# Five products of the self-attention and feed-forward parts in three rounded rounds, and w_down loaded later

## The reference

```python
x = x + xattn(layernorm(x), ctx_1024)      # q, k each layernormed by head, softmax, projection
x = x + attn(layernorm(x))                 # causal; scores plus 0.35 * tanh(Q) J tanh(K)
x = x + ffn(layernorm(x))

# attn: the three projections
Q = heads(Wq, bq); K = heads(Wk, bk); V = heads(Wv, bv)
# ffn: shared part and router
shared_out = silu(x @ shared_gate_w) * (x @ shared_up_w) @ shared_down_w
router_probs = softmax(x_flat @ router_w)
topk_probs, topk_idx = top_k(router_probs, 2)
# routed part: 16 experts, each silu(x @ g) * (x @ u) @ d, weighted by its probability
```

## Time and profile before

| | |
|---|---|
| timed executions | 1392.45, 1395.54, 1396.56 us; median 1395.54 us |
| the profiled execution's own time | 1382.54 us |
| its span (first to last instruction of the engines) | 1380.7 us |
| granted TensorE clock, mean over the span | 0.955 |
| PE busy | 1240.6 us (90%) |
| DVE busy | 984.4 us (71%) |
| ACT busy | 698.1 us (51%) |
| POOL busy | 450.4 us (33%) |

### The profile page before, as it was taken

The page is one execution under the profiler, slowest core; times in us unless marked ns, Lnnn a source line. Parts: engine busy times, 40 slices in busy tenths (PEclk is TensorE's granted clock), DMA queues, the critical chain, the costliest instruction groups (busy, mean ns, idle before and its releaser), DMA issues.

```text
span 1380.7 us, 54869 instructions
## 1 busy us (share of the span) xinstructions
PE 1240.6 (90%) x22808; PEld 1024.0 (74%) x22808; DVE 984.4 (71%) x2498; ACT 698.1 (51%) x1377; POOL 450.4 (33%) x436
## 2 busy tenths in 40 slices
PE   3789999999999999999999999999999986699950
PEld 3677878888888878788878787888888864488840
DVE  7458777777777777777777777777777763365547
ACT  1345555555555555555555555555555542255520
POOL 1322333333333333333333333333333222155530
PEclk7789999999999999999999999999999998699985
DMA  4100111111111111103111100111111002586558
GB/s 155 39 21 4 48 49 49 49 49 49 49 49 51 56 44 51 34 30 100 33 34 33 36 29 28 34 33 34 34 38 33 15 14 63 157 245 188 163 188 262
DMA packets 82579, 92.12 MB, mean 67 GB/s; under 512 B 17248, under 2 KB 72544, under 8 KB 82016
## 3 DMA queue, kind: packets, MB, share of 16 engines
q1 hardware_dynamic: 70816, 65.41, 16.4%
q0 software_dynamic: 6912, 19.01, 3.8%
q10 hardware_dynamic: 4608, 4.20, 0.9%
HBM read 61.19 MB, written 33.78 MB: 69 GB/s over the span
## 4 chain that ended last, share of the span: by engine, by line
PE 82%; DVE 9%; issue 4%; DMA 2%; ACT 1%; POOL 1%; SPq 0%; DVEq 0%; POOLq 0%; ACTq 0%
PE ringB L489 16%; PE ringC L500 14%; PE oA L582 10%; PE banksS L565 9%; DVE mx L1220 6%; PE banksS L783 5%; PE banksS L529 4%; PE ringB L663 3%; PE ringB L617 2%; PE ringB L649 2%; PE banksS L634 2%; PE ringB L484 2%; DMA out<-ksq 2%; PE oA L489 2%; PE banksS L544 2%
## 5 line engine op out<-in xcount | busy, mean ns | idle before, releaser
L863 ACT ACTIVATE pt<-banksS 128x1024 f32<-128x1024 f32 x128 | 127.7, 1023 | 129.6 <-PE banksS L565 118.0
L1039 POOL TENSOR_TENSOR kn<-kc,rr 128x512 f32<-128x512 f32 x64 | 66.6, 1062 | 336.0 <-DVE rr L1208 336.0
L500 PE MATMUL ringC<-wx_kv,ct 128*128 128x256 f32 x512 | 159.9, 312 | 13.6 <-DVE ws_down L1362 6.2
L1220 DVE TENSOR_REDUCE mx<-banksS 128x8 f32<-128x2048 f32 x64 | 146.3, 2287 | 0.9 <-PE banksS L544 0.9
L500 PE MATMUL ringC<-wx_kv_rest,ct 128*128 128x256 f32 x512 | 146.8, 287 | 0.0
L500 PE MATMUL ringC<-wx_kv,ct_rest 128*128 128x256 f32 x512 | 146.0, 285 | 0.0
L1033 POOL TENSOR_TENSOR sc<-sc,rz 128x1024 f32<-128x1024 f32 x32 | 62.3, 1948 | 223.5 <-DVE rz L1281 223.5
L565 PE MATMUL banksS<-qT,kT 17*128 17x64 f32 x4096 | 132.4, 278 | 0.9 <-DVE qT L1225 0.9
L565 PEld LDWEIGHTS banksS<-qT,kT 17*128 17x128 f32 x4096 | 123.5, 191 | 7.9 <-issue 1.4
L500 PEld LDWEIGHTS ringC<-wx_kv,ct 128*128 128x128 f32 x512 | 99.3, 194 | 27.6 <-DVE pos_u L1338 7.8
L1234 DVE RECIPROCAL rz<-oA 128x128 f32<-128x128 f32 x64 | 61.3, 957 | 55.5 <-PE oA L582 55.5
(11 more groups left out here) (219 smaller groups left out, 2957.0 us busy)
## 6 DMA issues: line engine op xcount, KB each, us to landing
ct_in<-in_ctxT SPq DMA_DIRECT2D x64, 256.0 KB, 3.1
pt<-rows_by_expert SPq DMA_DIRECT2D x80, 130.0 KB, 2.4
rows_by_expert<-in_pad_rows SPq DMA_DIRECT2D x16, 260.0 KB
xt<-in_x SPq DMA_DIRECT2D x32, 128.0 KB, 3.5
rows_without_experts<-base SPq DMA_DIRECT2D x32, 128.0 KB
pt<-expert_rows SPq DMA_DIRECT2D x16, 256.0 KB, 4.1
kn<-expert_rows SPq DMA_DIRECT2D x16, 256.0 KB, 4.2
out<-ksq ACTq DMA_DIRECT2D x32, 128.0 KB, 3.8
```

The lines of the kernel that those rows point to most:

```text
L500: mm = pe.matmul(ringC[:, half * DIM:(half + 1) * DIM], left[:, p, k, j // 2, (j % 2) * P:(j % 2 + 1) * P], right[:, k, part * DIM:(part + ...
L863: act.activation(pt[:, g, :, :, :, :].rearrange("p i q c n -> p i (q c n)"), banksS[:, :, g * 256:(g + 1) * 256], ACT.Exp)\
L1039: pool.tensor_tensor(kn[:, 2 * jj:2 * jj + 2, :, 0:HD].rearrange("p j h d -> p (j h) d"), kc[:, 2 * jj:2 * jj + 2, :].rearrange("p j (h d) ...
L1220: dve.tensor_reduce(mx[:, 2 * r:2 * r + 2, :, HD].rearrange("p q i -> p i q"), banksS[:, :, :].rearrange("p i (q m) -> p i q m", q=2), AX. ...
```

## The change

`x1T`, `hT`, `wa_qk`, `wa_v`, `w_route` and `ws_gu` become pairs of a rounded part (type fp32r) and a rest. The four products that read them (five weight matrices: q and k, v, the router, shared gate and up) go through `split_product`: six matmuls of fp32r instead of two of float32. DVE gets two new instructions in each step, `self_rows_rest` after `maxima` 0 and `ffn_rows_rest` after `key_sums` 1, which subtract the rounded rows from the PSUM bank. `free["NT"]` and `free["HT"]` are now raised by these; ACT's copy raises the new signals `rounded["NT"]` and `rounded["HT"]` on the same semaphore. The weights come into buffers used later (`sc`, `qkn`, `qk4`) and DVE splits them at the start of step 3. For the room, `w_down` now lies over `kn` and `kT`: SP loads it after the last use of these, in step 34, and DVE halves it in step 36. Rows that the last stage kept in `kn` and `kT` go elsewhere.

```diff
-        wa_qk = sb("wa_qk", [P, KD, 2 * DIM])
-        wa_v = sb("wa_v", [P, KD, DIM])
+        wa_qk, wa_qk_rest = (sb(n, [P, KD, 2 * DIM], F32R) for n in ("wa_qk", "wa_qk_rest"))
+        wa_v, wa_v_rest = (sb(n, [P, KD, DIM], F32R) for n in ("wa_v", "wa_v_rest"))
...
+        kn_kT = sb("kn_kT", [P, 2, 2048])
+        w_down = kn_kT[:, :, :].rearrange("p a (e d) -> p (a e) d", d=DIM)
...
+        rounded = {}
+        for u in ("NT", "HT"):
+            rounded[u], free[u] = Event(free[u].sem, 1, 2), Event(free[u].sem, 2, 2)
...
-                if 6 <= s < 18:
-                    load_expert_weights(s - 6)
+                if 6 <= s < 14:
+                    load_expert_weights(s - 2)
...
+                if s == TILES + 2:
+                    sp.wait_ge(full["C1"].sem, full["C1"].of(TILES - 1))
+                    for piece in range(4):
+                        load_expert_weights(piece)
...
+            def split_product(bank_, u, t, left, left_rest, source, right, right_rest, n):
+                pe.wait_ge(rounded[source].sem, rounded[source].of(t))
+                for r in (right, right_rest):
+                    for k in range(KD):
+                        pe.matmul(bank_[:, 0:n], left[:, k, :], r[:, k, 0:n], start=(r is right and k == 0), stop=False)
+                pe.wait_ge(free[source].sem, free[source].of(t))
+                for k in range(KD):
+                    mm = pe.matmul(bank_[:, 0:n], left_rest[:, k, :], right[:, k, 0:n], start=False, stop=(k == 1))
+                mm.then_inc(full[u].sem, 1)
...
-                product(bankB("QK"), "QK", lambda k: x1T[:, k, :], wa_qk, 2 * DIM)
+                split_product(bankB("QK"), "QK", b, x1T, x1T_rest, "NT", wa_qk, wa_qk_rest, 2 * DIM)
...
+            def self_rows_rest(b, p):
+                dve.wait_ge(rounded["NT"].sem, rounded["NT"].of(b))
+                freed(dve, full["QK"], b)
+                freed(dve, full["VP"], b)
+                dve.tensor_tensor(x1T_rest[:, :, :].rearrange("p k n -> p (k n)"), bankB("NT")[:, 0:DIM],
+                                  x1T[:, :, :].rearrange("p k n -> p (k n)").bitcast(F32), ALU.subtract).then_inc(free["NT"].sem, 1)
...
-                if s == TILES + 2:
+                if s == TILES + 4:
                     dve.wait_ge(expert_weights_in, 16 * 12)
                     dve.tensor_scalar(w_down[:, :, :], w_down[:, :, :], 0.5, None, ALU.mult).then_inc(weights_set, 1)
-                if s == 2:
+                if s == 3:
                     dve.wait_ge(self_weights_in, 16 * 7)
+                    split = ((wa_qk, wa_qk_rest, wa_qk_in), (wa_v, wa_v_rest, wa_v_in), (ws_gu, ws_gu_rest, ws_gu_in), (w_route, w_route_rest, w_route_in))
+                    for whole, _, source in split:
+                        ins = dve.tensor_copy(whole[:, :, :], source)
+                    ins.then_inc(setup_dve, 1)
+                    dve.wait_ge(setup_dve, 9)
+                    for whole, rest, source in split:
+                        dve.tensor_tensor(rest[:, :, :], source, whole[:, :, :].bitcast(F32), ALU.subtract)
                     dve.tensor_scalar(jmix[:, :, :], jmix[:, :, :], cols[:, 4:5], None, ALU.mult)
...
                 on(s, odd, 2, keys, 0)
                 on(s, odd, 3, maxima, 0)
+                on(s, odd, 4, self_rows_rest)
                 on(s, odd, 2, cross_normalised)
...
+                on(s, odd, 5, ffn_rows_rest)
                 on(s, odd, 2, queries)
```

More of the change, by code:

```diff
@@ L125, in perceiver_block @@
         w_gu = sb("w_gu", [P, KD, E, 2 * F])
-        w_down = sb("w_down", [P, E, DIM])
         wmean = sb("wmean", [P, KD, 3 * H])
@@ L163, in perceiver_block @@
         x1b = sb("x1b", [P, DIM])
-        x1T = sb("x1T", [P, KD, P])
+        x1T, x1T_rest = (sb(n, [P, KD, P], F32R) for n in ("x1T", "x1T_rest"))
         qkn = sb("qkn", [P, 2, H, PAD])
@@ L180, in perceiver_block @@
         h = sb("h", [P, 2, 2, ROW])
-        hT = sb("hT", [P, KD, P])
+        hT, hT_rest = (sb(n, [P, KD, P], F32R) for n in ("hT", "hT_rest"))
         th = sb("th", [P, DIM])
@@ L372, in load_self_weights @@
             def load_self_weights():
-                for dst, name in ((wa_qk, "wa_qk"), (wa_v, "wa_v"), (w_route, "w_route"), (ws_down, "ws_down")):
-                    load(dst[:, :, :], halves(name), self_weights_in)
-                load(ws_gu[:, :, 0:DIM], halves("ws_gate"), self_weights_in)
-                load(ws_gu[:, :, DIM:2 * DIM], halves("ws_up"), self_weights_in)
+                for dst, name in ((wa_qk_in, "wa_qk"), (wa_v_in, "wa_v"), (w_route_in, "w_route"), (ws_down[:, :, :], "ws_down")):
+                    load(dst, halves(name), self_weights_in)
+                load(ws_gu_in[:, :, 0:DIM], halves("ws_gate"), self_weights_in)
+                load(ws_gu_in[:, :, DIM:2 * DIM], halves("ws_up"), self_weights_in)
                 load(jmix[:, :, :], w["jmix"], self_weights_in)
@@ L640, in self_values @@
                 pe.wait_ge(free["NT"].sem, free["NT"].of(b))
-                product(bankB("VP"), "VP", lambda k: x1T[:, k, :], wa_v)
+                split_product(bankB("VP"), "VP", b, x1T, x1T_rest, "NT", wa_v, wa_v_rest, DIM)
             def probs_turned(b, p, g):
@@ L680, in route @@
                 claim(pe, B_USES, B_BANKS, "RT", d)
-                pe.wait_ge(free["HT"].sem, free["HT"].of(d))
-                product(bankB("RT"), "RT", lambda k: hT[:, k, :], w_route, E)
+                split_product(bankB("RT"), "RT", d, hT, hT_rest, "HT", w_route, w_route_rest, E)
             def counts(d, p):
@@ L1484, in _ @@
                     dve.wait_ge(out_done[c], 16 * (t // DEEP))
-                both = yg[q // DEEP][:, q % DEEP, :, :]
+                both = yg[q]
                 dve.scalar_tensor_tensor(res[:, c, :], both[:, 0, :], coef[:, t, 0:1], bases[t], ALU.mult, ALU.add)\
```

35 lines of the change are left out of this document (23 added, 12 removed).

## The result

The changed kernel takes 1520.76 us (1516.83 to 1530.14, 4 runs), the kernel before 1395.81 us beside it (1392.45 to 1396.56, 4 runs): a ratio of 1.091, 95% interval 1.086 to 1.096. It is 125 us slower. The prediction had said 63 us slower, 1459 us, with a range that ended at 1482. The direction was right, the size was half of it. The profiled execution of the changed kernel took 1520.51 us, its span is 1518.7 us, 138.0 us longer than that of before. The ratios in this document are estimated from the executions of both kernels, and differ by up to 0.002 from the ratio of the two medians beside them.

What follows compares the result with a forecast made beforehand. PE bounds the 29 steady steps. Gap less products +39 us, clock +22, start +2.8, step 4 -0.6: +63 us on 1395.5 gives 1459 us; own range 1444 to 1480, 8-in-10 range 1420 to 1482.

Steps and rivals of the forecast that it cites:

- The bound: In the 29 full steps PE is the bound, with 0.8 us idle per step; a new PE wait is paid almost in full.
- The gap: At O1, second half of the `pT`, `v` products, PE waits for DVE's subtraction emptying bank NT: 2.11 us per step lost.
- The second subtraction: DVE's `ffn_rows_rest` behind `key_sums` 1 is covered by DVE's idle time and score matmuls; otherwise 0.42 us per step lost.
- The products: Per step q and k gain 0.42 us, gate and up 0.42, values 0.15, router loses 0.23: 0.76 gained.
- the other end: Alternative price of a 512-column fp32r matmul, 0.24 us instead of the 0.215 taken; q and k then gain 0.27.
- the prediction's estimate from them: Three one-pass rounds against four float32 passes: a quarter less for every product shape, 1.17 us gained per step.
- The clock: Behind the gap at O1 the clock falls to 0.50 in half of the 29 steps, 1.5 us each: +22 us.
- the two cases of the earlier trace: PE idle stretches in the first steps: 1.90 us was followed by clock 0.50, 2.40 us kept 1.00.
- the clock falls in nearly every step: Rival: the clock falls behind the gap in nearly all 29 steps, 49 us for 22, total 1487 us; chance 0.06.
- a wait at O1 shorter than 0.76 us: Sign: with PE's wait at O1 below the products' gain of 0.76 us per step, the kernel gets faster.
- the prediction's second case: Rival: the gap at O1 comes but the clock stays, +41 us, 1437 us, between 1422 and 1447; chance 0.29.
- Start and end: Step 3's weight splitting costs +2.8 us, step 4 without O1 gains 0.6, the last steps with late `w_down` 0.

## Why the prediction was wrong

**The bound** was right: with the gap the 29 steps became longer by all of it and by the clock behind it. A step of before takes 997.5 / 29 = 34.4 us; the prediction's 34.1 came from a stretch that is not quite 29 steps long.

**The gap** was right in place, cause and size. Forecast 2.11 us per step, measured 1.93 to 1.97 in all 29; the subtraction took 0.41 us for the 0.42, the start followed its end within 0.06 us for the 0.15. The second subtraction is hidden as said: the router's maximum still waits for PE, 0.95 us at 793.26.

**The products** were mis-sized: 0.39 us per step for 0.76. Router (-0.23) and values (1.06 to 0.89, 0.17 for 0.15) came as forecast. Gate and up gained 1.89 - 1.57 = 0.32 for 0.42, q and k 1.71 - 1.58 = 0.13 for 0.42. Within a product two 512-column matmuls take 0.46 to 0.47 us, 0.233 each, near the other end that the prediction had named. The first two take more, 0.54 for gate/up behind the router and 0.65 for q and k behind a float32 product, and the last two of gate/up 0.56. The step took the price of a row of fp32r matmuls for that of six that stand among others. The Trainium skill counts four passes for float32 (FP8 and Floating Point Precision, true FP32); the prediction's estimate from them, 1.17 us per step, is farther off for this kernel's shapes than its own 0.76.

**The clock is the step that failed.** "One case for and one against gives half of the 29 steps, 15 x 1.5 = +22 us". It was 77 us. The price of a fall was right: 1.5 of 3.4 us is 0.44 per us, measured 0.49. The count was wrong, in two ways. First, the two cases of the earlier trace rows could not price this place. Both stood just ahead of the K0 product that closes a step, both ended with ACT's `va`, and both had twelve matmuls of 256 columns behind them; the gap here stands among 64x32 products. Yet their outcomes differ: 2.40 us kept the clock and 1.90 us lost it, and nothing in their surroundings says why. The trace before had more waits than these two. Here is one of two of 1.2 us that stood ahead of the narrow weighted sums, and then the rows around the other:

```profile
58.73 1.08 PE L582 MATMUL oA<-pt,va 128*32 128x64 f32 x32 [1.23 <-ACT pt L863]
```
```profile
91.00:92.10 1.10, 0.00 (x0) 0.00 (x1) 0.93 (x5) 1.10 (x2) 0.00 (x0) 1.00 0.00 0
...
95.00:102.40 7.40, 7.40 (x130) 6.96 (x127) 1.25 (x2) 2.07 (x3) 3.18 (x2) 0.50 0.31 92
```

Both lost the clock, for 10.2 us each (from 58.1 and from 92.3). A wait of 1.2 us at 1111.1, ahead of 16-row scores, and one of 1.5 us at 833.8, ahead of context matmuls, kept it. So no length of a wait separates the cases, and no count for a new place follows from them; the runs gave it. With the gap in every step at the same place, 28 and 29 of 29 steps fell where gate/up is float32, and in the changed kernel 19 behind the gap and the other 10 later. The 29 steps repeat the same work, and all or nearly all of them fell; half of them was a mean of two outcomes and not an outcome. Second, some falls are twice as long, and 22 stand where the prediction had nothing, 15 to 23 us into the step, in the rounded router and gate/up and behind them. With the long wait taken away 4 to 7 of these are left, with 0.34 us of it 15. The rival "the clock falls in nearly every step" was the true one (chance 0.06), and its 1487 (1486 by its own terms) was too low by the same error: it priced one fall per step.

One more reading of the prediction failed with it: that a wait at O1 shorter than 0.76 us makes the kernel faster. With 0.34 us it was 1.5% slower. The products gain 11 us in the 29 steps, the waits cost 10, the `issue` waits 8 and the later falls 25.

In the table "Why this matters for your kernels" of the Trainium skill (TensorE: Matmul & The Clock Gate) only longer gaps than this one are named as costing the clock, and the prediction's second case, 0.29, leaned on it beside the 2.40 us. The runs disagree: a float32 kernel with 1.92 us gaps fell in 28 of 29 steps.

**The issue waits** were not in the sum: +10 us. The profile before had them in small, 4.1 us in 11 waits. They do not simply grow with the rounded part: 2.9 to 4.3 us in the kernels with the gap alone, with the late `w_down` alone, with gate/up, and with q, k and values behind the gap; 6.9 to 9.9 in the other kernels without it; 11.7 with the gap of 0.34 us and 13.8 in the changed kernel. A part of them belongs to the later falls. In the changed kernel 15 of them, 5.7 us in all, last 0.37 to 0.39 us and end 6.5 to 7.1 us after the start of a later fall, as this one does after the fall at 829.2:

```profile
835.87 1.02 PE L607 MATMUL oA<-pt,head_ones 128*32 128x64 f32 x29 [0.37 <-issue]
```

What makes the rest is open; no run separates the length of the program from other causes.

**Start and end.** The start came to +4.1 for +2.8 - 0.6. The late `w_down` costs nothing that the timed executions show (ratio 1.001, 0.999 to 1.003). In step 36 DVE's scaling took 3.94 us and not 2.28, and its idle time still covers it:

```profile
1304.72 3.94 DVE L1395 TENSOR_SCALAR kn_kT<-kn_kT 128x4096 f32<-128x4096 f32 x1
1313.59 0.42 DVE L1311 TENSOR_TENSOR x<-ringB,x1b 128x256 f32<-128x256 f32 x1 [4.93 <-PE ringB L503]
```

The 6.1 us by which this profile's end is longer hold one more wait at O1 (1.6 us). The profile with only the late `w_down` has 4.0 us more there than before's, none of it in PE's listed waits; what they are stays open.

**Still open.** Why the kernels with the rounded router and gate/up lose the clock far more often in the later part of a step when O1 waits 0.34 or 1.94 us (15 and 22 times) than when it does not (4 to 7), although a wait of 0.4 us ahead of O0 leaves it at 6, and which of their matmuls does it. The counts of later falls are of one execution each.

## What to carry to other kernels

When a new instruction takes over the emptying of a bank, look first for who takes that bank next on the engine that is the bound; here it was not the product that the change was about, and two orders changed around it, or a copy that empties the bank at once, took back all of the 9%. A stall that stands in every step at the same place among narrow matmuls must be priced with the clock behind it; since the steps repeat each other, a mean over them can be far from every outcome. If no row of the trace has a wait in the same surroundings, a kernel with the stall alone gives the price: one dummy instruction did it here. Rounding pays for the products of 256 and 512 columns, not for 16: with the wait gone and the 16-column router left in float32 the kernel is 1.0% faster than before.
